# All sixteen batches of a transformer block written out, and keys moved ahead of queries on the DMA queue

## The chip, the cores and the metric

The kernel runs on one core of a Trainium2 chip. The metric is device time in microseconds of one execution. Three executions of the kernel before took 1717.52, 1721.43 and 1723.85 us (median 1721.43).

## What is computed

A block of a macaron transformer in float32 on `x` of shape (16, 512, 128): sixteen batches of 512 rows with 128 channels.

```python
x = x + 0.5 * ffn(layernorm(x), W_fc, W_proj)
x = x + attn(layernorm(x), w_qkv, w_out, b_out)
x = x + 0.5 * ffn(layernorm(x), W_fc, W_proj)
# attn: 16 heads of 64; scores q k^T / 8 + slope_h * -|i - j|, causal mask, softmax, times v, then w_out and b_out
# ffn: y = relu(x W_fc^T)^2 W_proj^T, then five steps of a spiking neuron:
#   mem = 0.9 * mem + y - (mem > 1), spike = mem > 1; the mean of the spikes is the result
```

## The kernel before

The batches go through one after the other. The sixteen heads of a batch are eight pairs, and a batch takes eight **slots**, s = 0 to 7, one for each pair. A slot has six **beats**, k = 0 to 5. In beat k of slot s TensorE computes the scores of one or two row tiles of pair s (`TILES`, head 1 in beats 0 and 1, head 0 from beat 2 on; lines 352 and 353), VectorE adds the position bias and takes the row extreme (L554), ScalarE takes the exponential (L795), VectorE the reciprocal of the row sums (L563), GpSimd normalises (L907). One slot later TensorE transposes the probabilities (`turn`, L366), ScalarE copies them out (L806), and two slots later TensorE multiplies them by the values (`pv`, L381). All else is side work that a table, `SIDE`, places on beats: the tiles of queries (`q`), keys (`k`) and values (`v`) of the next pair, the feed-forward blocks of the batch before and the batch after, and the output projection. Each line of `SIDE` is (slot, beat, kind, index, offset of the batch). All engines follow this order, written out by hand; semaphores with counted values tie them together, the values being functions of batch, pair and beat (`tile_no`, `pair_no`, `twice_no`, `keys_no`, lines 173 and on).

Queries and keys are split into a high half, rounded to the fast matmul type, and a low half, so that one matmul with 128 rows multiplies high and low halves of a head at once. For pair p + 1, side work of slot s = p: TensorE makes a tile in a bank (lines 336 to 338), ScalarE casts the high half (L823), VectorE subtracts to get the low half (L668 for queries, L675 for keys, into the single buffer `k_lo`). Then the halves must get to other partitions, which is done by six transfers of the SP queue in `place`, in this order:

- wait for the queries' low half (`s_qlo`), then two transfers of queries for head 1 (L292, 256 KB each, counted by `s_twice[par][1]`);
- wait for the keys' high half, then L295 (128 KB), wait for the low half, then L297 (128 KB); both counted by `s_keys[par][1]`;
- wait until the two L292 have landed, then L299, queries of head 0;
- wait until L295 and L297 have landed, then L302, keys of head 0.

TensorE waits for the transfers of head 1 in beat 0 and for those of head 0 in beat 2 (`scores`, lines 344 and 345). Before the next pair's `k_lo` is written VectorE waits for all transfers of keys of the pair before (L674). The lines of `SIDE` for queries and keys are:

```python
(0, 1, "k", 0, 0), (0, 1, "q", 0, 0),   (1, 1, "k", 0, 0), (1, 2, "q", 0, 0),
(2, 3, "q", 0, 0), (2, 3, "k", 0, 0),   (3, 0, "q", 0, 0), (3, 2, "k", 0, 0),
(4, 0, "k", 0, 0), (4, 0, "q", 0, 0),   (5, 0, "q", 0, 0), (5, 1, "k", 0, 0),
(6, 0, "k", 0, 0), (6, 1, "q", 0, 0),   (7, 1, "q", 0, 1), (7, 2, "k", 0, 1),
```

TensorE, VectorE, ScalarE and GpSimd each run the function `run`: batch 0 written out, a loop on the engine (`Fori`, L250) over batches 1 to 14 with two batches in its body, so seven passes, and batch 15 written out. The SP queue has its own loop (L323) over batches 1 to 12, six passes. Inside the loops the number of the batch is in a register; each semaphore value that depends on it is worked out by register instructions ahead of its wait. SP also loads the input of batch b + 2 (L274) at the start of batch b and stores the result of batch b - 1 (L279) at its end.

Of the kernel before, what the change touches and what calls it, by code (L numbers as in the profile page):

```python
# [7 lines left out]
F32 = mybir.dt.float32  # L8
F32R = mybir.dt.float32r

P = 128
B, N, C = 16, 512, 128
# [4 lines left out]
PAIRS = HEADS // 2  # L17
# [17 lines left out]
TRUNS = [[(1, 2), (0, 2)], [(1, 1), (1, 3)], [(0, 1), (0, 3)], [(1, 0)], [(0, 0)]]  # L35
TNEEDS = [max(SEG_TILE[h, i] for h, j in runs for i in range(j, NT)) for runs in TRUNS]
TRING = 8
TBEAT = [1, 2, 4, 5, 5]
ATTBEAT = 4
PV = [[], [], [], [], [0, 1, 2, 3], []]  # L40
PEORDER = ["DPT", "TPD", "TDP", "PTD", "TPD", "PTD"]
PVORDER = [j for js in PV for j in js]

PVLAST = [max(PVORDER.index(j) for _, j in runs) for runs in TRUNS]

# [33 lines left out]
def macaron_kernel(nc: bass.Bass, x, w_qkv, w_out, b_out, w_fc, w_proj, out):  # L79
    ctx = ExitStack()  # L80
    with ctx:
# [100 lines left out]
        def pair_no(b, p):  # L182
            return b * PAIRS + (p + 1)

        def twice_no(b, p, h):

            return (b * (PAIRS // 2) + (p // 2 + 1)) * (16, 32)[h]

        def keys_no(b, p, h):

            return (b * (PAIRS // 2) + (p // 2 + 1)) * (16, 32)[h]
# [16 lines left out]
        def before(b, p, back):  # L208

            return (b, p - back) if p >= back else (b - 1, p - back + PAIRS)  # L210

        def exists(b, p):
            return not isinstance(b, int) or (0 <= b < B)
# [31 lines left out]
        def run(eng, slot, head, tail):  # L245

            head()
            for s in range(PAIRS):
                slot(0, s, 0, (0, 1))
            with eng.Fori(1, B - 1, 2) as b:  # L250
                for ahead in range(2):
                    for s in range(PAIRS):
                        slot(b + ahead, s, (1 + ahead) % 2, (-1, 0, 1))
            for s in range(PAIRS):
                slot(B - 1, s, (B - 1) % 2, (-1, 0))
            tail()

        def side_at(s, k, offsets):

            s, k = (s, k) if k >= 0 else (s - 1, BEATS - 1)  # L260
            return [(n, kind, i, off, s) for n, (ss, kk, kind, i, off) in enumerate(SIDE)
                    if (ss, kk) == (s, k) and off in offsets]
# [4 lines left out]
        @block.sync  # L267
        def _(sp):
            xt = x.rearrange("b (t p) c -> b p t c", p=P)
            ot = out.rearrange("b (t p) c -> b p t c", p=P)  # L270

            def load_x(b, par):
                wait(sp, s_x1, b - 1)
                sp.dma_start(x_in[:, par, :, :], xt[b] if isinstance(b, int) else  # L274
                             xt[bass.ds(b, 1)].rearrange("b p t c -> (b p) t c")).then_inc(s_xin[par], 16)

            def store_x(b):
                wait(sp, s_x3, b + 1)
                sp.dma_start(ot[b] if isinstance(b, int) else  # L279
                             ot[bass.ds(b, 1)].rearrange("b p t c -> (b p) t c"), x3[:, :, :]).then_inc(s_stored, 16)  # L280

            def place(b, p):

                top, low = slice(0, DH), slice(DH, P)
                par = p % 2
                sp.wait_ge(s_qlo, pair_no(b, p))  # L290
                for rows in (top, low):
                    sp.dma_start(queries[rows, par, 1, :, :].bitcast(F32),  # L292
                                 queries[low, par, 0, :, :].bitcast(F32)).then_inc(s_twice[par][1], 16)
                sp.wait_ge(s_khi, pair_no(b, p))
                sp.dma_start(keys[top, par, 1, :].bitcast(F32), keys[low, par, 0, :].bitcast(F32)).then_inc(s_keys[par][1], 16)  # L295
                sp.wait_ge(s_klo, pair_no(b, p))
                sp.dma_start(keys[low, par, 1, :].bitcast(F32), k_lo[low, :].bitcast(F32)).then_inc(s_keys[par][1], 16)  # L297
                sp.wait_ge(s_twice[par][1], twice_no(b, p, 1))
                sp.dma_start(queries[low, par, 0, :, :].bitcast(F32),  # L299
                             queries[top, par, 0, :, :].bitcast(F32)).then_inc(s_twice[par][0], 16)  # L300
                sp.wait_ge(s_keys[par][1], keys_no(b, p, 1))
                sp.dma_start(keys[low, par, 0, :].bitcast(F32), k_lo[top, :].bitcast(F32)).then_inc(s_keys[par][0], 16)  # L302

            def slots(b, par, last):

                if last >= 2:
                    load_x(b + 2, par)
                for s in range(PAIRS):
                    if s < PAIRS - 1 or last >= 1:
                        place(*((b, s + 1) if s < PAIRS - 1 else (b + 1, 0)))  # L310
                if not isinstance(b, int) or b > 0:
                    store_x(b - 1)

            load_x(0, 0)
            sp.dma_start(fc_raw.rearrange("p (t c) -> p t c", c=C), w_fc.rearrange("(t p) c -> p t c", p=P)).then_inc(s_wfc, 16)
            sp.dma_start(proj_raw, w_proj).then_inc(s_wproj, 16)
            sp.dma_start(w_raw, w_qkv).then_inc(s_wqkv, 16)
            sp.dma_start(bias[:, :], b_out.rearrange("(a c) -> a c", a=1).to_broadcast([P, C])).then_inc(s_wo, 16)
            sp.dma_start(wo[:, :, :], w_out.rearrange("(m p) c -> p m c", p=P)).then_inc(s_wo, 16)
            load_x(1, 1)  # L320
            place(0, 0)
            slots(0, 0, 2)
            with sp.Fori(1, B - 3, 2) as b:  # L323
                for ahead in range(2):
                    slots(b + ahead, (1 + ahead) % 2, 2)
            for b in range(B - 3, B):
                slots(b, b % 2, min(2, B - 1 - b))
            store_x(B - 1)
            sp.wait_ge(s_stored, 16 * B)
# [3 lines left out]
        def _(pe):  # L333
# [52 lines left out]

            def qk_tile(dst, kind, b, p, par):

                if (p, kind) == (0, "q"):
                    pe.wait_ge(s_xlo[2], b + 1)  # L390
                hi, lo, done = (wq_hi, wq_lo, s_q) if kind == "q" else (wk_hi, wk_lo, s_k)
                cols = slice(p * P, (p + 1) * P)
                product3(dst, hi[:, cols], lo[:, cols], xa_hi[:, par, :], xa_lo[:, par, :]).then_inc(done, 1)
# [74 lines left out]
            def slot(b, s, par, offsets, between=None):  # L468
                t_of, pv_of = before(b, s, 1), before(b, s, 2)
                for k in range(BEATS):  # L470
                    if exists(b, s):
                        scores(b, s, k, par)
                    for part in PEORDER[k]:
                        if part == "P" and exists(*pv_of):
                            for j in PV[k]:
                                pv(*pv_of, j)
                        elif part == "T":
                            for t in range(len(TRUNS)):
                                if TBEAT[t] == k and exists(*t_of):
                                    turn(*t_of, t)  # L480
                        elif part == "D":
                            for n, kind, i, off, _ in side_at(s, k, offsets):
                                side(n, kind, i, off, b, s, par, last_user(n, b, offsets))
                    if between:
                        between(k)
# [298 lines left out]
        def _(act):  # L784
# [16 lines left out]
            def turned_out(b, p, t):  # L801
                act.wait_ge(s_turned, turn_no(b, p, t))

                bb, pp = before(b, p, 2 if t < 3 else 1)
                wait(act, s_pv, pv_no(bb, pp, PVLAST[t + 2 if t < 3 else t - 3]))
                act.copy(probT[:, turn_slot(p, t), :], turn_bank[(len(TRUNS) * p + t) % 2][:, :]).then_inc(s_turned_out, 1)  # L806

            def att_out(b, p, par):

                act.wait_ge(s_pv, pv_no(b, p, NT - 1))  # L810
                if p == 2:
                    wait(act, s_out, b * NT)
                act.copy(attT[:, att_at(p, par), :], pv_bank[:, :]).then_inc(s_att, 1)  # L813
# [44 lines left out]

            def slot(b, s, par, offsets):
                for k in range(BEATS):  # L860
                    for n, kind, i, off, ss in side_at(s, k - 1, offsets):
                        high_half(n, kind, i, b + off, ss, (par + off) % 2)
                    for t in range(len(TRUNS)):
                        if TBEAT[t] == k and exists(*before(b, s, 1)):
                            turned_out(*before(b, s, 1), t)
                    if k == ATTBEAT and exists(*before(b, s, 2)):
                        att_out(*before(b, s, 2), par if s >= 2 else 1 - par)
                    if exists(b, s):
                        exps(b, s, k)

            def chain(b, names):
                for n, (s, _, kind, i, off) in enumerate(SIDE):
# [114 lines left out]
```

## Time and profile before

| | |
|---|---|
| three runs, median | 1721.43 us |
| the profiled execution, its own time | 1727.58 us |
| its span | 1725.5 us |
| TensorE (PE) busy | 1606.9 us |
| ScalarE (ACT) busy | 1290.4 us |
| VectorE (DVE) busy | 1185.3 us |
| GpSimd (POOL) busy | 954.8 us |
| mean granted TensorE clock | 0.981 |
| moved by the SP queue's DMAs | 162.12 MB |

PE is TensorE's matmuls, PEld its weight loads, SPq and the like an engine's sequencer. In the rows a bracket at the end of a line is the idle time of the engine before that instruction, with what released it. [...] A row of busy time by stretch has the stretch, its length, the busy time (and number of instructions) of PE, PEld, DVE, ACT and POOL, then the granted clock, the DMA engines' busy share and GB/s. A stretch is given in microseconds from the start of the span; the slots of batch 2, for instance, begin at 245.57, 257.31 and 271.0 us.

### The profile page before, as it was taken

To read this page: it belongs to the slowest core of one execution; us is meant where nothing else is said; L and a number is where in the kernel's file an instruction comes from. 1 tells how busy PE (TensorE), PEld (TensorE's weight loads), DVE (VectorE), ACT (ScalarE), POOL (GpSimd) and SP (SyncE) were. 2 spreads that over 40 slices of the span, in tenths; PEclk is the share of its full clock that TensorE was granted. 3 is DMA by queue.
4 is the path that set the end of the run, shared out by engine and by line. 5 is a ranking of instruction groups with operands and counts; after the bars stand their busy time and mean duration, and the time that the engine had idled before them with its cause. 6 is when DMAs were issued, how large, how long until landed. Compare 5 with 4: busy or idle time off the path is not lost.

```text
span 1725.5 us, 39795 instructions
## 1 busy us (share of the span) xinstructions
PE 1606.9 (93%) x10902; PEld 1306.8 (76%) x10902; DVE 1185.3 (69%) x4272; ACT 1290.4 (75%) x3446; POOL 954.8 (55%) x1258
## 2 busy tenths in 40 slices
PE   4799999999999999989999899998999999999995
PEld 3677878778687877868778687877878778787774
DVE  6474785857768586775858758586785848768563
ACT  2588787878877787876878778787787868878781
POOL 3455565656556566555656556565565656656451
PEclk8899999999999999999999999999999999999998
DMA  2455453444544444544444444444443444545430
GB/s 75 89 111 117 93 113 84 95 97 100 108 98 97 91 102 97 111 94 87 88 101 100 97 102 105 92 102 97 101 106 83 102 97 93 114 87 107 93 83 13
DMA packets 80568, 164.90 MB, mean 96 GB/s; under 512 B 12880, under 2 KB 30928, under 8 KB 80208
## 3 DMA queue, kind: packets, MB, share of 16 engines
q1 hardware_dynamic: 80336, 162.12, 44.2%
q8 instruction: 107, 1.75, 0.4%
q14 instruction: 125, 1.02, 0.2%
HBM read 6.88 MB, written 4.19 MB: 6 GB/s over the span
## 4 chain that ended last, share of the span: by engine, by line
PE 61%; DVE 13%; DMA 11%; issue 7%; SPq 4%; ACT 2%; POOL 1%; DVEq 0%; ACTq 0%
DMA keys<-k_lo 11%; PE bank L381 9%; PE bank L366 9%; PE bank L424 7%; PE bank L352 7%; PE bank L432 6%; PE bank L353 6%; PE bank L336 5%; PE bank L337 5%; PE bank L338 5%; SPq L292 3%; DVE negsc L554 2%; DVE queries L668 2%; DVE drive L614 2%; SPq L295 1%
## 5 line engine op out<-in xcount | busy, mean ns | idle before, releaser
L907 POOL TENSOR_TENSOR prob<-prob,rsum 128x512 f32<-128x512 f32 (+3 forms) x1024 | 761.0, 760 | 705.6 <-DVE rsum L563 705.3
L795 ACT ACTIVATE prob<-negsc,negmax 128x512 f32<-128x512 f32 (+3 forms) x1024 | 573.6, 563 | 151.3 <-DVE negmax L554 144.6
L554 DVE CUSTOM_DVE_ANT_0 negsc<-bank,alibi 128x512 f32<-128x512 f32 (+3 forms) x1024 | 467.2, 475 | 7.1 <-PE bank L353 5.3
L352 PE MATMUL bank<-keys,queries 128*128 128x256 f32 (+2 forms) x1024 | 352.2, 355 | 68.8 <-DMA keys<-k_lo 58.6
L806 ACT COPY probT<-bank 128x512 f32<-128x512 f32 x640 | 361.0, 585 | 73.6 <-PE bank L366 72.7
L563 DVE RECIPROCAL rsum<-sums 128x1 f32<-128x1 f32 (+1 forms) x768 | 122.1, 159 | 411.7 <-PE bank L353 395.0
L366 PE MATMUL bank<-ident,prob 128*128 128x128 f32 x2560 | 367.7, 275 | 1.3 <-POOL prob L907 1.3
L366 PEld LDWEIGHTS bank<-ident,prob 128*128 128x128 f32 x2560 | 303.7, 141 | 27.7 <-issue 4.1
L353 PE MATMUL bank<-keys,queries 128*128 128x256 f32 (+2 forms) x1024 | 320.6, 327 | 0.0
L381 PE MATMUL bank<-probT,vals 128*64 128x512 f32 (+3 forms) x2048 | 303.9, 439 | 0.7 <-ACT probT L806 0.7
L352 PEld LDWEIGHTS bank<-keys,queries 128*128 128x128 f32 x1024 | 194.9, 190 | 102.9 <-issue 88.9
L381 PEld LDWEIGHTS bank<-probT,vals 128*64 128x64 f32 x2048 | 135.6, 136 | 159.7 <-issue 137.9
L353 PEld LDWEIGHTS bank<-keys,queries 128*128 128x128 f32 x1024 | 196.1, 191 | 13.5
L795 ACT ACTIVATION_READ_ACCUMULATOR prob<-negsc,negmax 128x1 f32 x1024 | 197.0, 192 | 0.0
L913 POOL TENSOR_TENSOR hid<-hid 128x512 f32<-128x512 f32 x128 | 142.6, 1125 | 13.6 <-ACT hid L848 13.3
L813 ACT COPY attT<-bank 128x512 f32<-128x512 f32 x128 | 75.2, 587 | 96.6 <-PE bank L381 96.2
L424 PE MATMUL bank<-wproj,hid 128*128 128x128 f32 x1024 | 129.6, 281 | 4.8 <-POOL hid L913 4.1
L424 PEld LDWEIGHTS bank<-wproj,hid 128*128 128x128 f32 x1024 | 121.7, 194 | 10.4 <-issue 4.3
L432 PE MATMUL bank<-wo,attT 128*128 128x128 f32 x960 | 117.0, 275 | 0.0
L432 PEld LDWEIGHTS bank<-wo,attT 128*128 128x128 f32 x960 | 113.1, 192 | 1.4 <-issue 0.2
L611 DVE SCALAR_TENSOR_TENSOR spikes<-negmem,spikes 128x512 f32<-128x512 f32 (+1 forms) x136 | 112.8, 835 | 1.0
L675 DVE TENSOR_TENSOR k_lo<-bank,keys 128x512 fp32r<-128x512 f32 x128 | 87.4, 683 | 20.7 <-ACT keys L823 20.4
(82 smaller groups left out, 2211.0 us busy)
## 6 DMA issues: line engine op xcount, KB each, us to landing
queries<-queries SPq DMA_DIRECT2D x384, 256.0 KB, 2.9
keys<-k_lo SPq DMA_DIRECT2D x256, 128.0 KB, 2.7
keys<-keys SPq DMA_DIRECT2D x128, 128.0 KB, 3.7
x_in<-in_L_attn_x_dram SPq DMA_DIRECT2D x16, 256.0 KB, 3.0
out_dram<-x SPq DMA_DIRECT2D x16, 256.0 KB, 2.5
prob<-in_L_attn_w_qkv_dram SPq DMA_DIRECT2D x1, 1536.0 KB, 8.5
wo<-in_L_attn_w_out_dram SPq DMA_DIRECT2D x1, 512.0 KB, 10.3
probT<-in_L_ffn_W_fc_dram SPq DMA_DIRECT2D x1, 256.0 KB, 3.3
```

The source lines that it names most:

```text
L352: pe.matmul(dst, q_hi[:, p % 2, h, rows], keys[:, p % 2, h, 0:width], start=True, stop=False)
L353: mm = pe.matmul(dst, q_lo[:, p % 2, h, rows], keys[:, p % 2, h, 0:width], start=False, stop=True)
L366: mm = pe.transpose(turn_bank[n % 2][:, col:col + P], prob[:, p % 2, h, PCOL[i] + j * P:PCOL[i] + (j + 1) * P], ident[:, :])
L381: mm = pe.matmul(pv_bank[h * DH:(h + 1) * DH, j * P:N], vals[:, (p // 2) % 2, j, (p % 2) * P + h * DH:(p % 2) * P + (h + 1) * DH], probT[: ...
L424: mm = pe.matmul(dst[:, t * C:(t + 1) * C], hid[:, i, rows], wproj[:, i, :], start=(i == 0 and t == 0), stop=(i == FC - 1), skip_group_che ...
L432: mm = pe.matmul(dst[:, 0:C], attT[:, att_at(m, par), t * P:(t + 1) * P], wo[:, m, :], start=(m == 0), stop=(m == PAIRS - 1))
L554: ins = dve.tensor_tensor_reduce(negsc[:, k % 3, col:col + WIDTH[i]], src, alibi[:, 2 * p + h, N - WIDTH[i]:N], 1.0, MASKED, ALU.add, ALU.min,
L563: dve.reciprocal(rsum[:, p % 2, cols], sums[:, p % 2, cols]).then_inc(s_rsum, 1)
L795: ins = act.activation(prob[:, p % 2, h, PCOL[i]:PCOL[i] + WIDTH[i]], negsc[:, k % 3, col:col + WIDTH[i]], ACT.Exp, bias=negmax[:, p % 2, ...
L806: act.copy(probT[:, turn_slot(p, t), :], turn_bank[(len(TRUNS) * p + t) % 2][:, :]).then_inc(s_turned_out, 1)
L907: ins = pool.tensor_tensor(pr, pr, rsum[:, p % 2, seg:seg + 1].to_broadcast([P, WIDTH[i]]), ALU.mult)
L913: pool.tensor_tensor(hid[:, i, :], hid[:, i, :], hid[:, i, :], ALU.mult).then_inc(s_hid[w], 1)
```

## The change

Two things are changed. The loops of all five engines become Python loops, so that every batch is written out and every batch number is a constant. And `place` issues the transfers of keys ahead of those of queries for the pairs whose keys' tile stands first in `SIDE` (pairs 1, 2, 5 and 7; `q_first` is true for 0, 3, 4 and 6): L295 and L297 before L292, L302 before L299. Besides, some tables get an index by slot with the same value in every slot, ScalarE's order within a beat is read from a table that holds the order it had, and TensorE waits for `s_xlo[2]` before the keys' tile of pair 0 too, which comes after the queries' tile that has that wait already.

```diff
-TBEAT = [1, 2, 4, 5, 5]
-ATTBEAT = 4
-PV = [[], [], [], [], [0, 1, 2, 3], []]
-PEORDER = ["DPT", "TPD", "TDP", "PTD", "TPD", "PTD"]
-PVORDER = [j for js in PV for j in js]
+TBEAT = [[1, 2, 4, 5, 5]] * PAIRS
+ATTBEAT = [4] * PAIRS
+PVBEAT = [4] * PAIRS
+PEORDER = [["DPT", "TPD", "TDP", "PTD", "TPD", "PTD"]] * PAIRS
+ACTORDER = [["STAE"] * BEATS] * PAIRS
+PVORDER = [0, 1, 2, 3]
...
-            with eng.Fori(1, B - 1, 2) as b:
+            for b in range(1, B - 1, 2):
...
+        def q_first(p):
+
+            return [kind for s, _, kind, _, _ in SIDE if s == (p - 1) % PAIRS and kind in "qk"] == ["q", "k"]
...
+                def low_queries():
+                    sp.wait_ge(s_qlo, pair_no(b, p))
+                    for rows in (top, low):
+                        sp.dma_start(queries[rows, par, 1, :, :].bitcast(F32),
+                                     queries[low, par, 0, :, :].bitcast(F32)).then_inc(s_twice[par][1], 16)
+
+                def low_keys():
+                    sp.wait_ge(s_khi, pair_no(b, p))
+                    sp.dma_start(keys[top, par, 1, :].bitcast(F32), keys[low, par, 0, :].bitcast(F32)).then_inc(s_keys[par][1], 16)
+                    sp.wait_ge(s_klo, pair_no(b, p))
+                    sp.dma_start(keys[low, par, 1, :].bitcast(F32), k_lo[low, :].bitcast(F32)).then_inc(s_keys[par][1], 16)
+
+                def top_queries():
+                    sp.wait_ge(s_twice[par][1], twice_no(b, p, 1))
+                    sp.dma_start(queries[low, par, 0, :, :].bitcast(F32),
+                                 queries[top, par, 0, :, :].bitcast(F32)).then_inc(s_twice[par][0], 16)
+
+                def top_keys():
+                    sp.wait_ge(s_keys[par][1], keys_no(b, p, 1))
+                    sp.dma_start(keys[low, par, 0, :].bitcast(F32), k_lo[top, :].bitcast(F32)).then_inc(s_keys[par][0], 16)
+
+                if q_first(p):
+                    low_queries()
+                    low_keys()
+                    top_queries()
+                    top_keys()
+                else:
+                    low_keys()
+                    low_queries()
+                    top_keys()
+                    top_queries()
...
-            with sp.Fori(1, B - 3, 2) as b:
+            for b in range(1, B - 3, 2):
...
-                if (p, kind) == (0, "q"):
+                if p == 0:
                     pe.wait_ge(s_xlo[2], b + 1)
...
```

## Rows read from the trace of the kernel before

**Rows 1.** The page, part 1: busy time and instructions of each engine.
```profile
PE 1606.9 (93%) x10902; PEld 1306.8 (76%) x10902; DVE 1185.3 (69%) x4272; ACT 1290.4 (75%) x3446; POOL 954.8 (55%) x1258
```

**Rows 2.** Busy time by stretch (columns above): batches 1 to 14; slot 1 of batch 7.
```profile
144.88:1585.45 1440.57, 1381.99 (x9464) 1126.14 (x9465) 1025.76 (x3695) 1123.87 (x3010) 832.89 (x1092) 0.99 0.46 98
...
775.75:789.93 14.18, 14.18 (x84) 11.54 (x84) 5.38 (x24) 10.21 (x27) 8.00 (x11) 0.88 0.38 79
```

**Rows 3.** Waits of TensorE in batches 1 to 14: us in total, times, longest.
```profile
PE bank L352 <- DMA keys<-k_lo: 56.4, 48, 3.3
```

**Rows 4.** TensorE's timeline: start us, us, instruction, [idle before it <-releaser].
```profile
234.20 0.49 PE L352 MATMUL bank<-keys,queries 128*128 128x512 f32 x1 [0.42 <-DMA keys<-k_lo]
...
245.57 0.49 PE L352 MATMUL bank<-keys,queries 128*128 128x512 f32 x1 [1.72 <-DMA keys<-k_lo]
...
257.31 0.49 PE L352 MATMUL bank<-keys,queries 128*128 128x512 f32 x1 [0.78 <-DMA keys<-k_lo]
...
261.12 0.49 PE L352 MATMUL bank<-keys,queries 128*128 128x512 f32 x1 [0.91 <-DMA keys<-k_lo]
...
349.06 0.49 PE L352 MATMUL bank<-keys,queries 128*128 128x512 f32 x1 [3.21 <-DMA keys<-k_lo]
```

**Rows 5.** The loop's line L250: instructions, min/median/max ns.
```profile
L250 PEldq COMPARE_BRANCH  x7: 83/4378/4414, 344.3 to 1582.3; - x7
```

**Rows 6.** Busy time by slot: 7, 0 (batch 2); 7, 0, 1 (batch 3).
```profile
234.20:245.57 11.37, 9.65 (x64) 7.47 (x65) 10.91 (x33) 9.56 (x27) 7.03 (x8) 1.00 0.52 108
245.57:257.31 11.74, 10.96 (x74) 8.69 (x75) 9.14 (x39) 10.01 (x30) 6.77 (x10) 1.00 0.65 146
...
336.17:349.06 12.89, 9.68 (x65) 7.50 (x65) 11.82 (x34) 10.33 (x30) 7.03 (x8) 1.00 0.51 107
349.06:362.00 12.94, 12.53 (x74) 9.99 (x75) 8.28 (x37) 8.83 (x23) 6.77 (x10) 0.87 0.53 120
362.00:374.60 12.60, 12.60 (x84) 10.26 (x84) 5.38 (x24) 11.27 (x33) 7.97 (x11) 1.00 0.48 99
```

**Rows 7.** Busy time of slot 3 in batch 14 and in batch 15.
```profile
1526.34:1537.41 11.07, 11.07 (x82) 9.15 (x81) 10.23 (x35) 8.74 (x26) 6.82 (x9) 1.00 0.49 103
...
1623.56:1634.73 11.17, 11.17 (x80) 9.23 (x81) 8.55 (x37) 7.30 (x20) 6.28 (x10) 1.00 0.50 106
```

**Rows 8.** SP's timeline: the last two transfers before slot 1 of batch 2.
```profile
255.77 0.46 SPq L299 DMA_DIRECT2D queries<-queries  x1
257.10 0.46 SPq L302 DMA_DIRECT2D keys<-k_lo  x1
```

**Rows 9.** Timelines of SP and TensorE at the start of slot 7, batch 0.
```profile
133.93 0.46 SPq L302 DMA_DIRECT2D keys<-k_lo  x1
...
134.00 0.47 PE L352 MATMUL bank<-keys,queries 128*128 128x512 f32 x1 [0.60 <-issue]
```

**Rows 10.** The page, part 3: an instruction queue: packets, MB, share.
```profile
q8 instruction: 107, 1.75, 0.4%
```

**Rows 11.** Line L302 (keys of head 0), its transfers.
```profile
DMA to landing us min/median/max: 2.2/2.3/4.1
```

**Rows 12.** Line L297 (low half of keys), its transfers.
```profile
DMA to landing us min/median/max: 2.2/3.7/5.1
```

**Rows 13.** VectorE's timeline: pair 7, slot 7, then pair 1.
```profile
223.12 0.69 DVE L675 TENSOR_TENSOR k_lo<-bank,keys 128x512 fp32r<-128x512 f32 x1 [0.66 <-ACT keys L823]
...
227.79 0.69 DVE L668 TENSOR_TENSOR queries<-bank,queries 128x512 fp32r<-128x512 f32 x1
...
234.96 0.17 DVE L563 RECIPROCAL rsum<-sums 128x2 f32<-128x2 f32 x1 [0.43 <-PE bank L353]
...
249.95 0.69 DVE L675 TENSOR_TENSOR k_lo<-bank,keys 128x512 fp32r<-128x512 f32 x1
...
250.55 0.68 DVE L668 TENSOR_TENSOR queries<-bank,queries 128x512 fp32r<-128x512 f32 x1
```

**Rows 14.** Line L292 (queries of head 1), its transfers.
```profile
DMA to landing us min/median/max: 2.9/3.6/4.6
```

More of the change, by code:

```diff
@@ L289, in place @@
                 par = p % 2
[L290 to L302, printed above, removed]
+                def low_queries():
[3 more added lines that the diff above has]
+                                     queries[low, par, 0, :, :].bitcast(F32)).then_inc(s_twice[par][1], 16)
@@ L472, in slot @@
                         scores(b, s, k, par)
-                    for part in PEORDER[k]:
-                        if part == "P" and exists(*pv_of):
-                            for j in PV[k]:
+                    for part in PEORDER[s][k]:
+                        if part == "P" and k == PVBEAT[s] and exists(*pv_of):
+                            for j in PVORDER:
                                 pv(*pv_of, j)
@@ L478, in slot @@
                             for t in range(len(TRUNS)):
-                                if TBEAT[t] == k and exists(*t_of):
+                                if TBEAT[s][t] == k and exists(*t_of):
                                     turn(*t_of, t)
@@ L860, in slot @@
                 for k in range(BEATS):
[L861 to L869, printed above, removed]
+                    for part in ACTORDER[s][k]:
+                        if part == "S":
+                            for n, kind, i, off, ss in side_at(s, k - 1, offsets):
+                                high_half(n, kind, i, b + off, ss, (par + off) % 2)
+                        elif part == "T":
+                            for t in range(len(TRUNS)):
+                                if TBEAT[s][t] == k and exists(*before(b, s, 1)):
+                                    turned_out(*before(b, s, 1), t)
+                        elif part == "A" and k == ATTBEAT[s] and exists(*before(b, s, 2)):
+                            att_out(*before(b, s, 2), par if s >= 2 else 1 - par)
+                        elif part == "E" and exists(b, s):
+                            exps(b, s, k)
             def chain(b, names):
```

## The prediction

> **What bounds the kernel now.** First the page: TensorE is busy 93% of the span, ScalarE 75%, the others less [rows 1]. So time is won only where TensorE stands still, and I looked for those places. Batches 1 to 14, which run in loops, take 1440.57 us, 102.9 each [rows 2]. TensorE's waits in that stretch are of one kind: the first score matmul of a pair (L352) waits 48 times, 56.4 us in all, for transfers of keys [rows 3]. TensorE's timeline says where [rows 4]: at the start of slot 7 (0.42 us), of slot 0 (1.72), of slot 1 (0.78), and inside slot 1 where head 0 begins (0.91). The last row of the group is the start of slot 0 right after the loop has jumped back: 3.21 us. By my count of such rows the 56.4 us are 32.6 at the starts of slot 0 (once 1.3, seven times 1.7, and 3.2 after each of six jumps), 11.7 at the starts of slot 1 (14), 6.0 inside slot 1 (six) and 6.1 at the starts of slot 7 (14). Everywhere else TensorE runs through.
>
> **Part 1, the loops written out.** Each engine jumps back six times; its seventh loop branch falls through. On TensorE a jump lasts about 4.4 us, the one that falls through 0.083 [rows 5]. The jump costs in two slots [rows 6]: slot 7 takes 12.89 us with it and 11.37 without, slot 0 takes 12.94 and 11.74. [...] The sum is 1.52 + 1.20 = 2.72 us, six times: **16.3 us**. Late next at this place is the ordinary start of slot 0 with its 1.7 us, as between the two batches inside the body, which are written out already; I take nothing off that.
>
> With constant batch numbers the register arithmetic falls away (1540 such instructions on TensorE's queue, 1848 on ScalarE's, by the trace's list). It is done ahead of the data nearly everywhere: slot 3 takes 11.07 us in batch 14, in the loop, and 11.17 in batch 15, which has constants already [rows 7]. I cost it at nothing there; what hides it is work still queued on the engine. Where the queue is empty it is bare: SP issues its last transfer of a pair (L302) upon the landing that also frees the score, and the score starts 0.21 us after that issue in the loop [rows 4, 8] and 0.07 after it in batch 0 [rows 9]. That is 0.14 us for each of 14 starts of slot 0: **2.0 us**.
>
> [...] A page can slow a transfer in flight: L302 has a median of 2.3 us to landing and a worst of 4.1 [rows 11]; the late ones are those inside slot 1, and a 16 KB packet flies beside each. [...]
>
> **Part 2, keys ahead of queries**, for pairs 1, 2, 5 and 7, where SIDE has the keys' tile first. Now SP issues two transfers of queries, then two of keys, the last of which lands 3.7 us after its issue [rows 12], and the score follows. The keys of pair 7 are ready (L675) 4.7 us before its queries (L668) [rows 13]: with the keys first, both key transfers are out by then. The number of transfers is the same; left behind the queries are two issues of queries and their landings. The queue shows when those are over: L299 waits for exactly them and is issued at 255.77, L302, which waits for the keys, at 257.10 [rows 8]; before pair 7 the two are 1.2 us apart. So pair 7 could start 1.2 us earlier. Its gap is 0.42 to 0.47: the whole gap goes and TensorE's own work sets the start, 14 x 0.44 = 6.1 us. VectorE can follow, since before its first operation of slot 7 it stood idle 0.43 us [rows 13], but no further: it is busy 11.82 of 12.89 us there [rows 6].
>
> Pair 1 is tighter, its k_lo being ready 0.6 us before its q_lo [rows 13]. TensorE would be ready at 256.53 (257.31 less 0.78 [rows 4]), and the queries have landed at 255.77 [rows 8]. The 14 starts sum to 11.7 us, all but two under 0.9; I take all. The second gap, inside slot 1, waits for L302, six times, 6.0 us. L302 now goes out once the keys have landed, some 3 us earlier; last are the top queries, issued at about 255.8, and a queries' transfer lands in 2.9 to 4.6 us [rows 14], so at 258.7 to 260.4, where head 0 would need them at 259.3. I take it as gone. Sum of the gaps: 11.7 + 6.0 + 6.1 = **23.8 us**. With the longest goes one stretch of low clock (slot 1 of batch 7: 14.18 us at 0.88 [rows 2], against 12.60 at 1.00 [rows 6]): **1.6 us**. Batches 0 and 15 have five more such starts (their rows repeat the pattern of [rows 4]), four of 0.6 to 0.9 us and one of 3.2; of that one about 1.2 goes, as before pair 7, of the others 2.8: **4.0 us**.
>
> The wait that this adds: SP stands at the keys' waits while queries could go. In these four slots the queries are never ready first, so nothing is held up behind it. Pairs 2 and 5 start without a gap in the loop: nothing won or lost.
>
> [...] First the rows: 128 KB of keys issued alone (L302) land in 2.3 us, as much behind the queries (L297) in 3.7 [rows 11, 12]; queued transfers wait for each other. [...] By the rows the first keys of pair 1 go out about 1.5 us before the first queries and land in 2.3, before the queries' 2.9 are over; I take the rows.
>
> **Sum.** 16.3 + 2.0 + 23.8 + 1.6 + 4.0 - 4.6 = 43.1 us. The profiled execution took 1727.58 us, its span is 1725.5, and the median of the three runs, 1721.43, is 6.2 lower; set against the median the forecast is **1678 us**. A measurement of this kernel tells a difference of about 0.5%, 8.6 us, from none.
>
> **Rivals.** (a) The queue decides: the queries of pair 1 land as late as the keys did. The starts of slot 1 and half of the gaps inside it stay: 1678 + 11.7 + 3.0 = 1693. For it: L297 against L302; against it: the 1.3 us between L299 and L302. (b) Reordering gives nothing, since VectorE, nearly full in slot 7, sets the pace; 16.3 + 2.0 - 4.6 remain, 1708 us. Against it: the idle 0.43 us. (c) More than forecast: VectorE and SP each save as much as TensorE (0.14 us) in the bare chain of slot 7, 3.9 us, and no page falls on a bare transfer, 4.6: 1670 us. [...] (e) The edit does nothing, as fetching stalls as often elsewhere and the bare transfers stay the same ones: 1721.
>
> **How the numbers follow.** Main case 0.66 (its own range 1670 to 1687: landing bounds, 0 to 8 page hits), (a) 0.13, (b) 0.06, (c) 0.09, (d) 0.03, (e) 0.03. The range leaves out (b), (d), (e) and the edges of the rest: 1666 to 1697. Faster: 0.66 + 0.13 + 0.06 + 0.09 = 0.94; same 0.03; slower 0.03.
>
> **What would show it.** Part 1: no loop branches and no register arithmetic, the start of slot 0 waiting 1.6 us in every batch, slot 7 near 11.3 us, the granted clock 1.00 from batch 1 to 14, fewer and evenly spaced instruction packets. Part 2: in slots 0, 1, 4 and 6 SP's key transfers before the queries'; no waits at the starts of slots 1 and 7, none inside slot 1; at slot 0 the releaser still the keys' transfer; batches of about 99.6 us. [...]

## The result, and the profile after

The changed kernel takes **1669.16 us** (median of four runs, 1666.16 to 1671.71) against 1721.54 for the kernel before: ratio 0.9697, 95% interval 0.9671 to 0.9724. The forecast was 1678, so 9 us more were won than I had summed up. The profiled execution took 1667.52 us. Two executions below, one of e4 (1986.45 us) and one of the kernel before beside it (2650.13 us), ran at a mean granted clock of 0.75 and 0.56 (here as everywhere a share of full speed) and stay out of the medians.

The page of the changed kernel, the same parts as read before:

```profile
span 1665.7 us, 34863 instructions
PE 1584.9 (95%) x10902; PEld 1293.9 (78%) x10902; DVE 1181.6 (71%) x4272; ACT 1284.4 (77%) x3446; POOL 955.3 (57%) x1258
...
q8 instruction: 90, 1.47, 0.4%
```

There are 34,863 recorded instructions where there were 39,795; the work of the engines is the same to the instruction. The packets of queue q8, 16,384 bytes each, are 90 where there were 107 [rows 10]. TensorE's two queues (PE and PEld) have 23,070 of the recorded instructions, 256 for each packet, and it is 256 in e1 too (23,054 for 90). So I take them for TensorE's code and call a packet a page of 256 of its instructions; that is an estimate from these counts. The lines have moved: L352 is now L375, L292 is L298, L295 and L297 are L303 and L305, L299 is L309, L302 is L314, L668 and L675 are L691 and L698.

The waits of TensorE in batches 1 to 14, after:

```profile
PE bank L375 <- issue: 22.7, 14, 1.9
PE bank L375 <- DMA queries<-queries: 1.9, 1, 1.9
```

Of 56.4 us [rows 3] 24.6 are left, 15 waits instead of 48. Fourteen are the ordinary start of slot 0, 1.26 us in batch 1 and 1.73 to 1.89 in the others (that the view calls most of them "issue" changes nothing: the first score matmul still waits for the keys' transfer, see below); the last is 0.39 us, inside slot 0 of batch 6. The waits at the starts of slots 1 and 7 and inside slot 1 are gone.

Busy time by stretch, after: slots 6, 7, 0, 1 around the start of batch 4, slot 4 of batch 4, then batches 1 to 14. The columns are those of the rows before the prediction.

```profile
415.84:429.65 13.81, 13.81 (x104) 11.50 (x101) 11.11 (x43) 10.41 (x29) 9.59 (x13) 1.00 0.31 68
429.65:441.08 11.43, 9.54 (x67) 7.39 (x65) 11.39 (x34) 10.05 (x28) 7.04 (x8) 1.00 0.49 104
441.08:451.91 10.83, 10.83 (x74) 8.69 (x75) 8.80 (x39) 9.04 (x27) 6.77 (x10) 1.00 0.69 160
451.91:464.48 12.57, 12.57 (x85) 10.06 (x84) 5.72 (x25) 11.71 (x34) 7.94 (x11) 1.00 0.44 95
492.85:504.12 11.27, 11.27 (x81) 9.15 (x80) 9.40 (x37) 10.94 (x30) 6.30 (x9) 1.00 0.53 116
143.94:1529.41 1385.47, 1360.40 (x9464) 1113.40 (x9465) 1022.45 (x3695) 1117.79 (x3010) 833.27 (x1092) 1.00 0.47 102
```

Against [rows 2, 6] the fourteen batches take 1385.47 us instead of 1440.57, 55.1 less, at a granted clock of 1.00; a batch takes 98.96 us. Slot 0 takes 10.83 us where it took 11.74, and 12.94 after a jump. In slots 6, 0, 1 and 4 the busy time of TensorE equals the length of the slot: it runs through. Slot 7 is now full on another engine: VectorE is busy 11.39 of 11.43 us (11.26 of 11.29 in most batches).

Slots 6, 7 and 4 of the kernel before at the same place, of which I had not read 6 and 4 for the prediction:

```profile
425.22:439.67 14.45, 14.04 (x103) 11.54 (x101) 11.68 (x44) 11.06 (x30) 9.59 (x13) 1.00 0.30 63
439.67:451.04 11.37, 9.66 (x65) 7.48 (x65) 10.92 (x33) 9.59 (x27) 7.03 (x8) 1.00 0.52 108
...
505.22:516.83 11.61, 11.49 (x80) 9.14 (x79) 9.57 (x37) 10.95 (x30) 6.22 (x9) 1.00 0.51 105
```

Slot 4 was 0.34 us longer in every one of the fourteen batches, with only 0.12 us of it idle. None of my terms covers it. The timelines of VectorE and TensorE in slot 4 of batch 4, before and then after, show where it was:

```profile
508.23 0.08 DVE L554 DVE_READ_ACCUMULATOR2_ANT negmax<- 128x1 f32 x1
508.71 0.69 DVE L675 TENSOR_TENSOR k_lo<-bank,keys 128x512 fp32r<-128x512 f32 x1 [0.39 <-ACT keys L823]
...
509.00 0.33 PE L353 MATMUL bank<-keys,queries 128*128 128x384 f32 x1
509.45 0.66 PE L408 MATMUL bank<-ident,xn 128*128 128x128 f32 x4
```

```profile
495.86 0.08 DVE L577 DVE_READ_ACCUMULATOR2_ANT negmax<- 128x1 f32 x1
495.97 0.69 DVE L698 TENSOR_TENSOR k_lo<-bank,keys 128x512 fp32r<-128x512 f32 x1
...
496.63 0.33 PE L376 MATMUL bank<-keys,queries 128*128 128x384 f32 x1
496.80 0.60 PE L431 MATMUL bank<-ident,xn 128*128 128x128 f32 x4
```

Before `k_lo` VectorE makes three waits (L671 and L674), each for a value worked out from the register, and it stood idle 0.39 us. The bracket names ScalarE, whose cast (L823) it waits for; but the trace puts the end of that wait at 508.50, and VectorE then runs two register instructions (at 508.52 and 508.62) and starts `k_lo` only at 508.71, 0.21 us after the signal. With constants it starts 0.02 us after the signal. The rest of the gap is ScalarE's: counted from the reciprocal before (L563, L586), its cast starts 0.17 us later in the kernel before. The transpose of `xn` (L408, now L431) writes the side bank that `k_lo` reads: it started 0.05 us after `k_lo`'s end and 0.45 us after the matmul ahead of it, now 0.17.

SP's timeline after: the transfers for pair 7, whose order is new, and for pair 0, whose order is old.

```profile
419.02 0.46 SPq L303 DMA_DIRECT2D keys<-keys  x1
419.75 0.46 SPq L305 DMA_DIRECT2D keys<-k_lo  x1
424.54 1.10 SPq L298 DMA_DIRECT2D queries<-queries  x2
425.68 0.62 SPq L314 DMA_DIRECT2D keys<-k_lo  x1
429.06 0.46 SPq L309 DMA_DIRECT2D queries<-queries  x1
435.37 1.10 SPq L298 DMA_DIRECT2D queries<-queries  x2
436.52 0.61 SPq L303 DMA_DIRECT2D keys<-keys  x1
437.18 1.24 SPq L305 DMA_DIRECT2D keys<-k_lo  x1
439.61 0.46 SPq L309 DMA_DIRECT2D queries<-queries  x1
441.00 0.46 SPq L314 DMA_DIRECT2D keys<-k_lo  x1
```

For pair 7 everything that slot 7 waits for has landed by 429.06 (L309's issue), and slot 7 starts at 429.65, when TensorE is through with slot 6. For pair 0 the keys land at 441.00 and slot 0 starts at 441.08, the 0.07 us of batch 0 [rows 9], and so in all fourteen batches.

### The profile page after: what moved, and what is told of

Read it like the earlier page. It is cut to its first block, busy times and chain, and to the rows that moved or that the text cites. A ratio compares the mean times of both kernels' runs of the same rounds, so it can differ in the third digit from the quotient of the medians.

```text
span 1665.7 us, 34863 instructions
## 1 busy us (share of the span) xinstructions
PE 1584.9 (95%) x10902; PEld 1293.9 (78%) x10902; DVE 1181.6 (71%) x4272; ACT 1284.4 (77%) x3446; POOL 955.3 (57%) x1258
## 4 chain that ended last, share of the span: by engine, by line
PE 78%; DVE 11%; DMA 4%; issue 4%; POOL 1%; ACT 1%; SPq 1%; DVEq 0%
PE bank L404 13%; PE bank L389 13%; PE bank L375 8%; PE bank L376 8%; PE bank L359 7%; PE bank L447 7%; PE bank L455 6%; PE bank L360 6%; PE bank L361 6%; DMA queries<-queries 4%; DVE drive L637 2%; DVE negsc L577 2%; DVE spikes L634 2%; DVE queries L691 1%; DVE negmem L640 1%
## 5 line engine op out<-in xcount | busy, mean ns | idle before, releaser
L375 PE MATMUL bank<-keys,queries 128*128 128x256 f32 (+2 forms) x1024 | 346.7, 350 | 34.5 <-issue 25.5
L586 DVE RECIPROCAL rsum<-sums 128x1 f32<-128x1 f32 (+1 forms) x768 | 121.4, 158 | 353.5 <-PE bank L376 336.1
L389 PE MATMUL bank<-ident,prob 128*128 128x128 f32 x2560 | 364.0, 273 | 1.3 <-POOL prob L933 1.3
L376 PE MATMUL bank<-keys,queries 128*128 128x256 f32 (+2 forms) x1024 | 318.3, 325 | 0.0
L375 PEld LDWEIGHTS bank<-keys,queries 128*128 128x128 f32 x1024 | 193.8, 189 | 61.6 <-issue 38.4
L698 DVE TENSOR_TENSOR k_lo<-bank,keys 128x512 fp32r<-128x512 f32 x128 | 87.2, 681 | 17.9 <-ACT keys L846 17.3
```

The lines of the kernel that those rows point to most:

```text
L375: pe.matmul(dst, q_hi[:, p % 2, h, rows], keys[:, p % 2, h, 0:width], start=True, stop=False)
L376: mm = pe.matmul(dst, q_lo[:, p % 2, h, rows], keys[:, p % 2, h, 0:width], start=False, stop=True)
L389: mm = pe.transpose(turn_bank[n % 2][:, col:col + P], prob[:, p % 2, h, PCOL[i] + j * P:PCOL[i] + (j + 1) * P], ident[:, :])
```

## The experiments

All times are medians; each ratio is to the kernel before on the same chip. The kernels of this table shared one chip, where the kernel before had a median of 1722.87 us. e4, e5, e6 and e8 ran on a second one (kernel before 1723.95), e9 and e10 on a third (1720.23). The changed kernel did not run there, so these are set against it by their ratios and by batches 1 to 14 of the traces.

| kernel | us | ratio, 95% interval | batches 1 to 14 in the trace |
|---|---|---|---|
| before | 1722.87 | | 1440.57 |
| e3: one pass, numbers in registers | 1711.57 | 0.9935, 0.9909 to 0.9961 | 1418.75 |
| e1: written out, old order | 1692.74 | 0.9826, 0.9796 to 0.9857 | 1404.90 |
| e2: loops, new order | 1700.43 | 0.9880, 0.9848 to 0.9911 | 1418.94 |
| after | 1669.12 | 0.9695, 0.9666 to 0.9723 | 1385.47 |

The last column is from the profiled execution of each; that of e3 was the fastest of its eight (1703.84 us), so its trace flatters it, and the kernel before has the trace that the rows come from (1727.58 us).

**The changed kernel again, as e0,** for a sum of the parts on one chip.

> The changed kernel itself, on the same chip as the other three, so that they can be compared with it: 1669 us, ratio 0.970. If the parts add up, the gains of e1 and e2 sum to its gain within 3 us; if one makes room for the other, its gain is larger than the sum.

Measured 1669.12 us, 53.7 below the kernel before. How the two parts add up to it stands under e2.

**e1, the loops alone.** In the kernel before:

```diff
-            with eng.Fori(1, B - 1, 2) as b:
+            for b in range(1, B - 1, 2):
...
-            with sp.Fori(1, B - 3, 2) as b:
+            for b in range(1, B - 3, 2):
```

> The kernel before with all loops written out and nothing else: SP's order of transfers stays queries, keys in every slot. My account of the 52 us: six jumps 16 us, register arithmetic about 7 us (0.14 us at each start of slot 0 and 0.34 us in each slot 4), the rest by the order of transfers. Expected 1721 - 23 = 1698 us, with the starts of slots 7 and 1 still waiting 0.3 to 0.7 us for keys, slot 4 at 11.27 us and the granted clock near 1.00 in batches 1 to 14. Rival: the pages of instructions, fetched at fixed places of every pass and in bursts at a jump, made the transfers late; with the loops gone they are in time and the order adds little: 1685 us or less.

Measured 1692.74 us, 30.1 below the kernel before, between the account's 1698 and the rival's 1685. The starts of slots 7 and 1 still wait, slot 4 has 11.27 us. Its waits of TensorE in batches 1 to 14:

```profile
PE bank L352 <- issue: 37.3, 47, 1.7
PE bank L352 <- DMA queries<-queries: 1.7, 1, 1.7
```

And its busy time by stretch, slots 6, 0 and 4 around batch 4:

```profile
424.36:438.61 14.25, 13.98 (x103) 11.50 (x101) 11.56 (x44) 10.84 (x30) 9.60 (x13) 1.00 0.30 62
...
449.98:461.27 11.29, 11.00 (x75) 8.67 (x75) 9.11 (x39) 9.45 (x26) 6.78 (x10) 1.00 0.66 148
...
502.15:513.42 11.27, 11.27 (x80) 9.15 (x79) 9.41 (x37) 10.94 (x30) 6.30 (x9) 1.00 0.52 109
```

There are as many waits as before, 48, but none is longer than 1.7 us, and those at the starts of slots 7 and 1 are 0.28 us in most batches, where they were 0.44 at slot 7 and in most batches 0.78 or 0.42 at slot 1. The order of transfers is still worth 1692.74 - 1669.12 = 23.6 us on top, so the rival, by which it adds little, is out.

**e2, the order alone.** The changed kernel with `Fori` in both places, as before.

> The kernel after with its loops back on the engines, so the new order of transfers alone. My account: 24 us of waits plus what the pipeline overlap at those starts adds (0.16 us each) and batches 0 and 15, less nothing: 1721 - 29 = 1692 us; six idle stretches of TensorE of about 3.2 us stay, each with a stretch of low clock, slot 4 stays at 11.61 us. Rival (the pages): 1710 us or more, since the order adds little while jumps disturb the transfers.

Measured 1700.43 us, 22.4 below. The rival's 1710 lies above, my 1692 below it. The jumps stay (six starts of slot 0 wait 3.4 us), and slot 4 has its 11.61 us. The 8 us that it is short of my account are in part the clock: eight slots 0 run at a granted clock of 0.86 to 0.88, among them those of batches 8, 10 and 12, which no jump precedes. Slot 0 of batch 6, and of batch 8, both after a start that waited 1.90 us:

```profile
643.41:654.18 10.77, 10.77 (x74) 8.71 (x75) 8.79 (x39) 9.05 (x27) 6.76 (x10) 1.00 0.69 161
846.24:858.61 12.37, 12.37 (x75) 10.05 (x75) 8.88 (x39) 9.33 (x27) 6.77 (x10) 0.86 0.60 140
```

That is 1.6 us a slot, 4.8 in three, which neither the kernel before nor the changed kernel loses there. What decides it is not shown. The two parts add up to 30.1 + 22.4 = 52.5, and both together give 53.7 on this chip. The sum fits, but the parts do touch each other: with the loops written out there is less of each gap left for the order to take, and with the loops kept the order loses some of its gain to the clock.

**e3, no jumps but registers.** In the kernel before:

```diff
-            with eng.Fori(1, B - 1, 2) as b:
-                for ahead in range(2):
+            with eng.Fori(1, B - 1, B - 2) as b:
+                for ahead in range(B - 2):
...
-            with sp.Fori(1, B - 3, 2) as b:
+            for b in range(1, B - 3, 2):
```

> The kernel before with a loop of a single pass on four engines, its body batches 1 to 14, SP written out. Batch numbers stay in registers, so the register arithmetic stays and no engine jumps back. This parts the jumps from the arithmetic. My account: 1721 - 16 = 1705 us, slot 4 still 11.61 us, slot 0 still starts 0.21 us after SP's L302 is issued. Rival: a written-out body alone gives all that e1 gives, 1698 or less, and the arithmetic costs nothing.

Measured 1711.57 us, 11.3 below the kernel before (6.7 to 15.7 by the interval) where I expected 16. The trace shows one branch, which falls through, no start that waits longer than 2.2 us, and slot 4 as it was, beside slots 6, 7 and 0. SP's numbers are constants in e3 too, so its 11.3 us hold SP's share of the arithmetic along with the jumps:

```profile
L250 PEldq COMPARE_BRANCH  x1: 96/96/96, 1560.5 to 1560.5; - x1
```

```profile
421.07:435.56 14.49, 14.03 (x104) 11.53 (x101) 11.73 (x44) 11.10 (x30) 9.59 (x13) 1.00 0.30 63
435.56:446.94 11.38, 9.66 (x64) 7.48 (x65) 10.89 (x33) 9.53 (x27) 7.04 (x8) 1.00 0.51 107
446.94:458.34 11.40, 10.93 (x74) 8.68 (x75) 9.13 (x39) 9.67 (x28) 6.77 (x10) 1.00 0.65 149
...
499.28:510.89 11.61, 11.49 (x81) 9.14 (x80) 9.57 (x37) 10.96 (x30) 6.24 (x9) 1.00 0.50 104
```

Between e3 and e1 the batch numbers on the four engines become constants and nothing else is edited. That is worth 1711.57 - 1692.74 = **18.8 us**, more than the jumps. What can be seen of it slot by slot is 0.24 us in slot 6 (14.49 to 14.25), 0.11 in slot 0, 0.34 in slot 4 and, in most batches, 0.17 in slot 7 (11.38 to 11.21): about 0.86 us a batch, 12 us in fourteen; batches 1 to 14 of the two traces differ by 13.9. The part in slots 6, 7 and 0 is the chain that starts a pair: the first score follows SP's L302 by 0.21 us in e3 at the starts of slots 7, 0 and 1, and by 0.07 in e1. The rest of the 18.8 is not located, and that it belongs to the arithmetic is not shown: the two programs also differ in length (94 packets of TensorE's code and 90), and both have bare transfers that can be late. Nor is all of it won in the changed kernel, where the starts of slots 7 and 1 wait no more. There slot 4's 0.34 us and, against e2, 0.16 in slot 7 (11.45 to 11.29) and 0.06 in slot 6 can be seen, 7.8 us in fourteen batches.

**e4 and e5, one pair each back to the old order.** In the changed kernel, `if q_first(p) or p == 1:` and `if q_first(p) or p == 7:`.

> The changed kernel with pair 1 alone back to queries before keys. By my account each start of slot 1 waits again: slot 0 is 11.27 us instead of 10.82, 14 x 0.45 = 6 us, and one to three late L302 inside slot 1 cost 1.4 us each: 1669 + 9 = 1678 us. If the queue's order ate the gain (keys in front delay the queries), slot 0 changes by less than 0.1 us and the time stays 1669.

Measured 1676.31 us (ratio 0.9727, 0.9689 to 0.9765, against 0.9695): 5.5 us lost by the ratios, whose intervals overlap, and 6.8 by the traces (batches 1 to 14 take 1392.26 us, 1385.47 in the changed kernel), where I expected 9. Slot 0 of batch 4, with TensorE idle again for its last part:

```profile
439.09:450.38 11.29, 10.99 (x75) 8.67 (x75) 9.13 (x39) 9.47 (x27) 6.79 (x10) 1.00 0.65 148
```

That is 11.29 us against 10.83, and about so in every batch: the queue's order does not eat the gain of pair 1.

> The changed kernel with pair 7 alone back to queries before keys. My account: slot 6 is 14.26 us instead of 13.83, of which slot 7 gives 0.1 back (11.21 instead of 11.31), since VectorE is nearly full there: 14 x 0.33 = 5 us, 1674 us. If VectorE set the pace of slots 6 and 7, the sum of both slots stays 25.1 us and the time 1669.

Measured 1677.86 us (0.9733, 0.9700 to 0.9765): 6.5 lost by the ratios and 7.9 by the traces (1393.38 us), where I expected 5. Slots 6 and 7 around batch 4:

```profile
416.60:430.87 14.27, 13.99 (x103) 11.49 (x102) 11.57 (x45) 10.86 (x30) 9.59 (x13) 1.00 0.30 62
430.87:442.24 11.37, 9.63 (x65) 7.48 (x65) 11.08 (x33) 9.73 (x28) 7.03 (x8) 1.00 0.53 111
```

In most batches slot 6 is 14.28 and slot 7 11.21, 25.49 against 25.12 in the changed kernel, 5.2 us in fourteen; the rest are single late transfers, as in slot 0 of batch 14 with 12.25 us. A start that bare transfers set is open to those too. Singly the two pairs give 12 to 15 us, where the order as a whole gives 23.6 with the loops written out (19.4 in the traces). Pairs 2 and 5 were not tested singly.

**e8, a try to shift the pages.** The kernel of e1 with `keep_warm(64)` added at the end of TensorE's `head`, meant to move all later page ends by half a page; one execution.

> [...] If pages in flight are what makes single transfers late, the long slots of e1 (slot 1 of batches 1 and 3 with 13.99 us, slot 6 of batch 2 with 15.54) return to 12.55 and 14.26 us and others become long, about as many. If something else does it, the same slots stay long.

Measured 1703.96 us. In e1 the second wait of slot 1 in batch 1 came with L302 in flight beside a TensorE page; the timeline of that stretch, and the view of what its DMA queues carried meanwhile:

```profile
158.12 0.46 SPq L302 DMA_DIRECT2D keys<-k_lo  x1
...
162.30 0.47 PE L352 MATMUL bank<-keys,queries 128*128 128x512 f32 x1 [1.23 <-issue]
```

```profile
q8 instruction: 1, 0.02, 2.4%
...
keys<-k_lo SPq DMA_DIRECT2D x1, 128.0 KB, 4.1
```

One batch later, without such a page, the same transfer took 2.2 us. In e8 slot 6 of batch 2 is back to 14.27 us. Slot 1 of batch 1 is shorter but not ordinary (13.29 us; its L302 takes 3.4 us, again with a page beside it), and slot 1 of batch 3 is long for another reason (14.11 us at a granted clock of 0.88, behind a new wait of 1.77 us at its start). New long waits are those 1.77, 1.33 inside slot 7 of batch 2, 1.31 inside slot 0 of batch 7 and 0.90 inside slot 1 of batch 8. But slot 6 of batch 13 and slot 0 of batch 14 are long in both kernels (15.06 and 12.39 us in e1, 15.16 and 12.75 in e8). But the ends of pages did not move against the program. The call puts 128 weight loads and 128 matmuls in the trace (L466 stands there 206 times in each list, 78 in e1), 256 recorded instructions more, and q8 has 91 packets to e1's 90: a whole page, not the half I had meant to add. Counted in TensorE's recorded instructions, with 256 added to e1's, 76 of the 90 packets start within 20 instructions of the same place in both kernels. So e8 cannot tell whether the place of page ends makes transfers late, and what makes the long slots differ is not shown. What the traces do show is a count in e1: of the 768 transfers of `place`, 21 took over 0.8 us longer than is usual at their place, and 18 of these had a 16 KB packet in flight; 100 others had one too and were not late. In the kernel before it is 26 of 26, with 87 others. (The run's time is above e1's by 11 us, of which 7 lie ahead of batch 1, where the added matmuls are; one execution says no more.)

**e6, a try at what is left.** In the changed kernel the tiles of pair 0 stand a beat earlier:

```diff
-    (7, 0, "v", 1, 0), (7, 1, "q", 0, 1), (7, 2, "k", 0, 1),
+    (7, 0, "v", 1, 0), (7, 0, "q", 0, 1), (7, 1, "k", 0, 1),
```

> The changed kernel with the queries' and keys' tiles of pair 0 each one beat earlier in slot 7 (beats 0 and 1). What is left of TensorE's waits is 1.74 us at each start of slot 0, the chain tile, halves, four transfers. If that chain sets it, the wait goes and the time falls by 15 x 1.7 = 25 us to 1644 us. If VectorE's work in slot 7 (10.9 of 11.3 us) sets it, little is won: slot 7 stays over 10.9 us or TensorE waits for VectorE in slot 0 instead, 1662 us or more.

Measured 1677.40 us (0.9726, 0.9694 to 0.9759), slower than the changed kernel by 5.3 us by the ratios and 7.6 by the traces (1393.05 us). The wait at slot 0 is gone and comes back inside it. Slots 7 and 0 around batch 4, TensorE's wait, GpSimd ahead of it, and VectorE at that time:

```profile
431.04:441.09 10.05, 9.60 (x67) 7.44 (x65) 9.14 (x26) 8.10 (x22) 4.58 (x7) 1.00 0.51 107
441.09:453.93 12.84, 11.31 (x78) 8.55 (x76) 11.09 (x47) 10.98 (x32) 8.85 (x12) 1.00 0.62 144
```

```profile
443.20 0.65 PE L389 MATMUL bank<-ident,prob 128*128 128x128 f32 x4 [1.07 <-POOL prob L933]
...
440.78 2.37 POOL L933 TENSOR_TENSOR prob<-prob,rsum 128x512 f32<-128x512 f32 x2 [1.30 <-DVE rsum L586]
...
440.55 0.15 DVE L586 RECIPROCAL rsum<-sums 128x1 f32<-128x1 f32 x1
...
444.40 0.16 DVE L586 RECIPROCAL rsum<-sums 128x2 f32<-128x2 f32 x1
```

Slot 7 is now 10.05 us long, less than VectorE's work in it (11.26 us in the changed kernel). VectorE comes to one of slot 7's last reciprocals at 440.55, behind its spike steps; GpSimd, which stood idle 1.30 us for it, is through with two tiles at 443.15, and TensorE, whose slot 0 began at 441.09, waits 1.07 us for GpSimd. VectorE's first reciprocal of slot 0 comes at 444.40, 3.3 us after the slot's start (1.0 in the changed kernel). Both slots take 22.9 us together instead of 22.3 in the changed kernel's batch 4.

**e9 and e10, pair 0 keys first.** The last line of `SIDE` becomes `(7, 0, "k", 0, 1), (7, 1, "q", 0, 1)` in e9 and `(7, 1, "k", 0, 1), (7, 1, "q", 0, 1)` in e10, and with it `q_first(0)` turns false.

> The changed kernel with the keys' tile of pair 0 in beat 0 of slot 7, its queries' tile still in beat 1, and so its keys' transfers first too. After the queries' low half two transfers are left instead of four, so slot 0 can start about 1.0 us earlier, and no work of TensorE or VectorE is added. If the chain of transfers sets it, slots 7 and 0 together take 21.1 us instead of 22.1 and the time is 1669 - 14 = 1655 us. If VectorE's queue sets it, as in e6 (slots 7 and 0 together 22.8 us), they stay at 22 us or more and the time at 1669 or above.

> As e9, but with the keys' tile in beat 1 just ahead of the queries' tile, so that VectorE gets both subtractions in one beat, 0.7 us later for the queries than now. Transfers alone would give 0.3 us a batch, 1665 us; if VectorE's order decides, the queries' low half is late by a whole beat's work and the time is 1669 us or more.

Measured 1677.14 us (0.9747, 0.9729 to 0.9766) and 1674.08 us (0.9727, 0.9710 to 0.9745): neither is faster than the changed kernel. e9 is slower by 9 us by the ratios and 10 by the traces (1395.42 us), e10 by 5.5 and 4.5 (1389.99 us), with intervals that overlap for e10. VectorE in slot 7 of e9:

```profile
432.17 0.72 DVE L640 SCALAR_TENSOR_TENSOR negmem<-negmem,drive 128x512 f32<-128x512 f32 x1
433.79 0.17 DVE L586 RECIPROCAL rsum<-sums 128x2 f32<-128x2 f32 x1 [0.90 <-PE bank L376]
```

The earlier tile of keys has to wait for its side bank (TensorE stands 0.45 us for ScalarE's copy of the values in front of it), beat 1's scores come later, and VectorE, which was the full engine of this slot, stands idle 0.90 us. The start of slot 0 waits 1.13 us instead of 1.74 in most batches, and yet slot 7 takes 11.38 us (11.29 in the changed kernel) and slot 0 11.48 (10.83). What makes slot 0 longer I have not located. No version of mine beats the changed kernel; by e6, what would have to shrink first is VectorE's work in slots 7 and 0, which was not tried.

## Why the prediction was right, point by point

**What bounds the kernel** was read rightly: the waits at the starts of slots 0, 1 and 7 were what could be won, and all but the ordinary start of slot 0 went, as forecast. That start waits about 1.75 us; I had said 1.6. A batch takes 98.96 us; the 99.6 that I named does not follow from my own sum, which gives 100.1 for batches 1 to 14. By terms, part 1 was forecast at 16.3 + 2.0 - 4.6 = 13.7 us and gave 30.1 (e1), and part 2 was forecast at 23.8 + 1.6 + 4.0 = 29.4 and gave 23.6 (e1 against the changed kernel). The first was 16 us too small and the second 6 too large. That the total came within 9 us of the measured time is partly luck: the two errors have opposite signs.

**The jumps, 16.3 us.** Their place holds: none of the long starts is left once nothing jumps, and from batch 1 to 14 the granted clock is 1.00. In the kernel before slot 0 behind a jump ran at 0.82 to 0.89, six times; in batch 3 the clock was 0.50 from 350 to 353 us and 1.00 from 354 us on. A wait as long does not always bring it: in e2 slot 0 of batch 3 ran at 1.00 behind 3.39 us. The price of the jumps was a little high: e3 measured 11.3 us (6.7 to 15.7). That 16.3 less the 4.6 for pages makes 11.7 is not a proof, since the pages were counted for one bare transfer a batch and e3 has three; late transfers cost it about 1 us each, in slot 6 of batch 14 for instance (15.71 us instead of 14.51). Only TensorE's jump is long, 4.4 us; the branches of VectorE, ScalarE, GpSimd and SP (which jumps five times, not six) last 0.04 to 0.06.

**The register arithmetic, 2.0 us, is the term that was most mis-sized.** The 0.14 us at the start of slot 0 are there as forecast (0.21 us to 0.07 after SP's last issue, in all fourteen batches). The zero for all else was wrong: I took slot 3 for all slots, and there it costs nothing that can be seen (11.07 us with registers, 11.17 with constants [rows 7]). Between e3 and e1 it is up to 18.8 us, of which the traces locate 12. It costs at the starts of slots 7 and 1 too, in the old order, and where an engine has several waits in a row in front of an instruction that others wait for: in slot 4, 0.34 us a batch, at VectorE's `k_lo`. A comparison of slot 4 in batch 14 and batch 15 would have shown just this before the change (11.61 against 11.28 us, at equal busy time of ScalarE and less of VectorE); the prediction does not make it.

**Pages, 4.6 us lost.** No run shows this term, an estimate of mine from 88 pages, a bare transfer in 3.7 us of 100 and 1.4 us a hit; it took the size of an instruction as given, which no row had shown. The runs have 90 pages and no such loss in the changed kernel. That late transfers have a page beside them holds (26 of 26 in the kernel before, 18 of 21 in e1, and L302's 4.1 against 2.2 us), and around each of the six jumps three packets start, about 3.6 us ahead of the branch and 2.1 and 5.1 after its start. But in the changed kernel's trace none of TensorE's packets flies beside the transfers of pair 0 for longer than their first 0.3 us. The start of slot 0 is late by 0.15 us in two batches, and the 0.39 us wait inside slot 0 of batch 6 is behind a transfer (L314, 3.25 us instead of 2.27) with no instruction packet beside it; its cause stays open.

**Keys first, 23.8 us of waits, 1.6 of clock and 4.0 in batches 0 and 15.** Forecast 29.4 us, measured 23.6 with the loops written out (e1 to after) and 22.4 with the loops kept (e2). Pair 1 gave 6 to 7 and pair 7 6 to 8 (e4, e5). The account holds: the whole of the gap goes, and TensorE's work then sets the start (slots 6 and 0 are busy for all of their 13.81 and 10.83 us). What I missed is that both parts take from the same gaps: written out, those at the starts of slots 7 and 1 and inside slot 1 are 14.9 us in e1's batches 1 to 14 instead of 23.8. And a slot shrinks by more than its listed gap (slot 6 from 14.27 to 13.82 us and slot 0 from 11.29 to 10.83 for gaps of 0.28), 0.16 us at each of 28 starts, 4.5 us; the two together are about the 19.4 us by which the traces of batches 1 to 14 differ. The lead of the queries was a little under the 1.2 us that I read: L309 is issued 4.5 us after the first L298, as against 4.3 for L299 after L292, and 0.59 us before slot 7 starts.

**VectorE** limited slot 7 as I had written: with the gap gone it is busy 11.39 of 11.43 us, and slot 7 gave back about 0.1 us (11.21 in e1, 11.3 after).

**The rivals.** (a), that the queue's order eats pair 1's gain, is refuted by e4: for pair 1 the two queries need 4.55 us from the first issue to their landing in the changed kernel and 4.28 in e4 (medians of the batches), while the keys behind them cost 1.25. Even of these 0.27 us little is due to the keys ahead, since pair 7, whose keys have landed long before, shows 4.49. The keys ahead, issued 1.4 and 0.6 us earlier, land 2.1 and 1.3 us before the first of the queries. (b), that VectorE sets the pace already, was wrong for this change and right for the next one tried (e6). (c) named the right number, 1670 against 1669, but only half of the reason: no page fell on a transfer of pair 0 beyond its first 0.3 us, yet the chain ahead of slot 0 became shorter by 0.16 us and not by three times 0.14. (d), slower, with a stall of TensorE at each page end, and (e), nothing, are out: batches 1 to 14 have 78 packets and only 15 waits, all ahead of a first score matmul (L375).

## What to carry to other kernels

Where a loop's body is long and every semaphore value comes from a register, look for instructions with two or three such waits in a row on a busy engine; a written-out body with constants can give as much as the jumps themselves (here 12 us located, against 11.3). A start that waits for several transfers is set by the operand that is ready last: queue the others ahead of it, and expect about the gap (here 0.45 us a slot for listed gaps of 0.28). Two changes that shorten the same gap do not each get it whole, so a sum of terms needs the gap that the other change leaves. Before moving more work ahead, look at which engine is full in that slot.

## What the runs showed that I had not expected

The step from registers to constants was worth 18.8 us in fourteen batches (12 of them located), against 11.3 for six jumps of 4.4 us each. Late transfers mostly have a page of code beside them (18 of 21 in e1): a 128 KB transfer took 4.1 us with one 16 KB instruction packet beside it and 2.2 without. Low clock can follow an ordinary wait too: behind one of 1.9 us slot 0 ran at 1.00 in four batches of e2 and at 0.86 in three others. The spread of the times became smaller as well: on the chip of the table thirteen runs of the kernel before lie between 1713.21 and 1730.36 us, six of the changed one between 1667.99 and 1670.80. That the fewer bare transfers are the cause of this calm was not tested.
